# Attention scores on 128 rows: high and low parts of q stacked over k twice, the maximum as one more row

## What is computed

```python
q = conv1x1(Wq)      # (8, 12, 64, 1024)
k = conv1x1(Wk)
v = conv1x1(Wv)
scores = jnp.einsum('bhdn,bhdm->bhnm', q, k) * scale
attn = jax.nn.softmax(scores, axis=-1)
out = jnp.einsum('bhnm,bhdm->bhdn', attn, v)
out = out.reshape(B, C, H, W)
return jnp.einsum('oc,bchw->bohw', Wp, out)
...
x = x + _L0_conv_ref(_gn(x), L0_conv_Wq, L0_conv_Wk, L0_conv_Wv, L0_conv_Wp)
```

## Time and profile before

| | |
|---|---|
| median of 3 runs | 3721.03 us (3720.8 to 3722.98) |
| profiled execution | 3720.18 us |
| its span, first to last instruction | 3718.4 us |
| PE busy in the span | 95% |
| POOL, DVE, ACT busy in the span | 48%, 39%, 31% |
| DMA queue q1, share of 16 engines | 37.1% |
| HBM | 266 MB read, 206 MB written |

### The profile page before, as it was taken

One profiled execution on the slowest core, in us unless ns is written; L12 is line 12 of the kernel. 1 busy time (PEld: TensorE's weight loads), 2 busy tenths in 40 slices (PEclk: granted clock), 3 DMA queues, 4 the chain that ended last, 5 costly groups with the idle time before them and its releaser, 6 DMA issues.

```text
span 3718.4 us, 52007 instructions
## 1 busy us (share of the span) xinstructions
PE 3543.5 (95%) x18800; PEld 2342.1 (63%) x18800; DVE 1443.6 (39%) x1787; ACT 1160.4 (31%) x2017; POOL 1803.1 (48%) x772
## 2 busy tenths in 40 slices
PE   3999999999999888899999999999999999999996
PEld 3888988888889744445555555555555555555555
DVE  4333333233332154444444444444444444444421
ACT  2111111111111034444444444444434444444340
POOL 0000000000000058887777777787777777778770
PEclk7999999999999989999999999999999999999998
DMA  4333324323333332244343443433433434434325
GB/s 188 136 132 124 131 101 145 142 101 133 116 135 105 122 137 92 92 137 137 126 148 112 140 148 114 140 115 116 144 132 131 145 106 148 140 115 139 120 70 169
DMA packets 264948, 476.07 MB, mean 128 GB/s; under 512 B 60704, under 2 KB 110112, under 8 KB 263712
## 3 DMA queue, kind: packets, MB, share of 16 engines
q1 hardware_dynamic: 264736, 473.27, 37.1%
HBM read 265.95 MB, written 206.44 MB: 127 GB/s over the span
## 4 chain that ended last, share of the span: by engine, by line
PE 60%; issue 2%; ACT 2%; DVE 1%; DMA 0%; POOL 0%; POOLq 0%; ACTq 0%; SPq 0%
PE psum L712 23%; PE psum L725 19%; PE psum L745 12%; PE psum L697 5%; ACT p_all L807 2%; PE psum L736 1%; DVE half_max L850 0%; POOL sums L674 0%; DMA k<-k_parts 0%; DMA k<-o_parts 0%; POOL o L657 0%; DMA o_parts<-o_lo 0%; POOLq L409 0%; DMA top<-neg_max 0%; ACTq L806 0%
## 5 line engine op out<-in xcount | busy, mean ns | idle before, releaser
L674 POOL TENSOR_TENSOR sums<-sums,p_all 128x1024 f32<-128x1024 f32 x576 | 1357.8, 2381 | 204.5 <-ACT p_all L807 204.5
L850 DVE TENSOR_REDUCE half_max<-psum 128x2 f32<-128x1024 f32 x768 | 940.4, 1226 | 1266.8 <-PE psum L697 1266.8
L807 ACT ACTIVATE p_all<-psum 128x512 f32<-128x512 f32 x1536 | 834.3, 595 | 1149.1 <-PE psum L712 1140.6
L674 POOL TENSOR_TENSOR sums<-p_all 128x1024 f32<-128x1024 f32 x96 | 226.0, 2375 | 1625.7 <-ACT p_all L807 1625.7
L712 PE MATMUL psum<-q,k 64*128 64x512 f32 x4608 | 742.8, 427 | 52.3 <-ACT p_all L807 50.3
L725 PE MATMUL psum<-p_all,v 128*64 128x512 f32 x3072 | 743.4, 605 | 0.0
L712 PEld LDWEIGHTS psum<-q,k 64*128 64x128 f32 x4608 | 375.2, 185 | 511.7 <-issue 278.8
L745 PE MATMUL psum<-a,wp 128*128 128x512 f32 x1620 | 465.1, 416 | 0.0
L225 PE MATMUL psum<-xn_hi,w_hi 128*128 128x512 f32 x1152 | 449.9, 391 | 5.6 <-DVE xn_lo L334 5.5
L225 PE MATMUL psum<-xn_lo,w_hi 128*128 128x512 f32 x1152 | 449.0, 390 | 0.0
L225 PE MATMUL psum<-xn_hi,w_lo 128*128 128x512 f32 x1152 | 449.0, 390 | 0.0
(11 more groups left out here) (55 smaller groups left out, 2032.3 us busy)
## 6 DMA issues: line engine op xcount, KB each, us to landing
q_parts<-stage SPq DMA_DIRECT2D x192, 256.0 KB, 2.1
k_parts<-stage SPq DMA_DIRECT2D x192, 256.0 KB, 2.3
q<-q_parts SPq DMA_DIRECT2D x48, 1024.0 KB, 6.3
k<-k_parts SPq DMA_DIRECT2D x48, 1024.0 KB, 8.9
a<-o_parts SPq DMA_DIRECT2D x90, 512.0 KB, 5.0
x_raw<-in_x SPq DMA_DIRECT2D x8, 3072.0 KB, 11.2
v_rows<-stage SPq DMA_DIRECT2D x128, 192.0 KB, 2.1
v<-v_rows SPq DMA_DIRECT2D x48, 512.0 KB, 4.2
```

The costliest lines, as they stand in the source:

```text
L674: pool.tensor_tensor(sums[:, m % 2, i, :], first, p_all[:, i, n, :], ALU.add).then_inc(added, 1)
L807: act.activation(p_all[:, i, (m * MT + t) % EXPS, h * BANK:(h + 1) * BANK], scores[:, r, :], ACT.Exp, scale=SCALE).then_inc(exp_done, 1)
L850: dve.tensor_reduce(half_max[:, :, t, h], of, AX.X, ALU.max, negate=True).then_inc(max_done, 1)
```

## The change

Each head gets 128 rows. `q_both` holds the high part of q on 64 rows and the low part on the other 64; `k_twice` holds the high part of k on both; one product of the two gives high k by high q plus high k by low q. `k_low` holds the low part of k on one half, zeros on the other half, and ones in one row of that half; `q_top` holds the high part of q on the same half, zeros on the other, and the maxima in that one row. Their product gives low k by high q plus the maximum. A K block is now 4 matmuls on all 128 rows, 2 for one head, then 2 for the other, and each head waits for its own score bank.

U keeps its form (64 rows a head; the heads' tiles are now `q_top` and `k_twice`), and moves: in steps 2 to 6 one unit stands between the second K and V and one behind V. O stands between the two K blocks without a unit, except in step 7, where a unit splits it. S moves ahead of V. `sums` has one buffer. q and k are loaded by eight DMAs a pair in place of two (3 MB in place of 2 MB), the parts of `lo` one pair ahead, with two slots. At the start DVE sets the zero halves and the rows of ones.

```diff
-    UNITS_BY_STEP = ((1, 1, 1),) + ((0, 1, 1),) * 6 + ((0, 1, 0),)
+    UNITS_BY_STEP = ((1, 1, 0, 1, 0), (0, 0, 0, 0, 1)) + ((0, 0, 0, 1, 1),) * 5 + ((0, 0, 1, 1, 0),)
...
-                ch = bass.ds(p * P, P)
-                sp.dma_start(f32(q[:, e, :, :]), q_dram[:, ch, :].rearrange("s p n -> p s n")).then_inc(qk_in[e], 16)
-                sp.dma_start(f32(k[:, e, :, :]), k_dram[:, ch, :].rearrange("s p n -> p s n")).then_inc(qk_in[e], 16)
+                for i, part in enumerate(half_of):
+                    sp.dma_start(f32(q_top[part, e, i, :]), q_dram[0, bass.ds(p * P + i * DH, DH), :]).then_inc(hi_in[e], 16)
+                for part in half_of:
+                    sp.dma_start(f32(k_twice[part, e, :, :]),
+                                 k_dram[0, bass.ds(p * P, P), :].rearrange("(i c) n -> c i n", i=2)).then_inc(hi_in[e], 16)
+
+            def load_lo(p, e, scored):
+
+                wait(sp, s_ready, scored)
+                for s, part in enumerate(half_of):
+                    sp.dma_start(f32(q_both[part, e, :, :]),
+                                 q_dram[s, bass.ds(p * P, P), :].rearrange("(i c) n -> c i n", i=2)).then_inc(lo_in[e], 16)
+                for i, part in enumerate(half_of):
+                    sp.dma_start(f32(k_low[part, e, i, :]), k_dram[1, bass.ds(p * P + i * DH, DH), :]).then_inc(lo_in[e], 16)
...
                         if t == 1:
-                            wait(pool, sums_ready, p - 1)
+                            wait(pool, sums_ready, p)
...
-                wait(pe, exp_done, n + 2 - RING)
                 cols, keys = slice(h * BANK, (h + 1) * BANK), slice(t * P, (t + 1) * P)
-                for c in range(4):
-                    for i, part in enumerate(half_of):
-                        r = ((m * MT + t) * 4 + 2 * h + i) % RING
-                        left, right = ((k[part, e, 0, keys], q[part, e, 0, cols]), (k[part, e, 0, keys], q[part, e, 1, cols]),
-                                       (k[part, e, 1, keys], q[part, e, 0, cols]), (ones_r[part, :], top[part, e, cols]))[c]
-                        mm = pe.matmul(scores[:, r, :], left, right, start=(c == 0), stop=(c == 3))
-                        if c == 3:
-                            mm.then_inc(s_ready, 1)
+                for i, c in ((0, 0), (1, 0), (0, 1), (1, 1)) if first else ((0, 0), (0, 1), (1, 0), (1, 1)):
+                    r = ((m * MT + t) * 4 + 2 * h + i) % RING
+                    if c == 0:
+                        wait(pe, exp_done, n + i + 1 - RING)
+                    if first and (i, c) == (0, 1):
+                        pe.wait_ge(top_in, 32 * (p + 1))
+                    left, right = ((k_twice[:, e, i, keys], q_both[:, l, i, cols]),
+                                   (k_low[:, l, i, keys], q_top[:, e, i, cols]))[c]
+                    mm = pe.matmul(scores[:, r, :], left, right, start=(c == 0), stop=(c == 1))
+                    if c == 1:
+                        mm.then_inc(s_ready, 1)
...
                 for t in range(MT):
+                    front, behind, middle, late, end = units(t)
+                    maxima(front)
                     if t == 0 and not first:
                         values(p - 1, m - 1, None, MT - 1)
+                    maxima(behind)
+                    scores_by_key(p, m, u, t, 0)
...
+                        output(small, n % KT, share[:2], count)
+                    maxima(middle)
+                    if at_least(p, LAG):
+                        output(small, n % KT, share[2:], count)
+                    scores_by_key(p, m, u, t, 1)
+                    maxima(late)
+                    if t == SUMS_AT and not first:
+                        add_up(p - 1, m - 1, (p + 1) * UNITS + sum(map(sum, UNITS_BY_STEP[:t])) if not last else NP * UNITS)
                     if t > 0:
                         values(p, m, u, t - 1)
+                    if t == SUMS_AT:
+                        wait(pe, sum_copied, p)
+                    maxima(end)
...
-            dve.memset(f32(ones_r[:]), 1.0).then_inc(set_done, 1)
-            dve.memset(f32(top[:]), 0.0).then_inc(set_done, 1)
+            for i in range(2):
+                other, row = half_of[1 - i], slice((1 - i) * DH, (1 - i) * DH + 1)
+                dve.memset(f32(q_top[other, :, i, :]), 0.0).then_inc(set_done, 1)
+                dve.memset(f32(k_low[other, :, i, :]), 0.0).then_inc(low_zero, 1)
+                dve.wait_ge(low_zero, i + 1)
+                dve.memset(f32(k_low[row, :, i, :]), 1.0).then_inc(set_done, 1)
```

More of the change, by code:

```diff
@@ L422, in attend_phase @@
         p_all = sb("p_all", [P, 2, EXPS, N])
[L423 removed]
+        sums = sb("sums", [P, 2, N])
         half_max = sb("half_max", [P, 2, MT, 2])
@@ L505, in units @@
             done = sum(map(sum, UNITS_BY_STEP[:t]))
-            first, second, third = UNITS_BY_STEP[t]
-            return (range(done, done + first), range(done + first, done + first + second),
-                    range(done + first + second, done + first + second + third))
-        SETS = 3
+            ends = [done + sum(UNITS_BY_STEP[t][:n]) for n in range(6)]
+            return [range(a, z) for a, z in zip(ends, ends[1:])]
+        SETS = 5
         block = ctx.enter_context(nc.Block())
@@ L692, in scores_by_query @@
                 if unit == 0:
-                    pe.wait_ge(qk_in[e], 32 * (turn(p, m, u) + 1))
+                    pe.wait_ge(hi_in[e], 64 * (turn(p, m, u) + 1))
                 wait(pe, max_done, p * UNITS + unit if taken is None else taken)
                 for i, part in enumerate(half_of):
-                    queries = q[part, e, 0, :].rearrange("p (n t) -> p t n", t=MT)[:, t, :]
-                    mm = pe.matmul(to[:, i, :], queries, k[part, e, 0, h * BANK:(h + 1) * BANK], start=True, stop=True)
+                    queries = q_top[part, e, i, :].rearrange("p (n t) -> p t n", t=MT)[:, t, :]
@@ L698, in scores_by_query, with scores_by_key @@
+                    mm = pe.matmul(to[:, i, :], queries, k_twice[part, e, i, h * BANK:(h + 1) * BANK], start=True, stop=True)
                 mm.then_inc(rows_ready, 1)
-            def scores_by_key(p, m, t, h):
-                e = m % SLOTS
-                if t == 0 and h == 0:
-                    pe.wait_ge(top_in, 32 * (p + 1))
+            def scores_by_key(p, m, u, t, h):
+                e, l = m % SLOTS, m % Q_SLOTS
+                first = t == 0 and h == 0
+                if first:
+                    pe.wait_ge(lo_in[l], 64 * (turn(p, m, u, Q_SLOTS) + 1))
@@ L735, in add_up @@
                         c, cols = 2 * i + h, slice(h * BANK, (h + 1) * BANK)
-                        mm = pe.matmul(totals[c * QUARTER:(c + 1) * QUARTER, :], ones[:], sums[:, m % 2, i, cols], start=True, stop=True)
+                        mm = pe.matmul(totals[c * QUARTER:(c + 1) * QUARTER, :], ones[:], sums[:, i, cols], start=True, stop=True)
                 mm.then_inc(sums_ready, 1)
@@ L877, in pair @@
                 for t in range(MT):
-                    begun, early, late = units(t) if not last else ((), (), ())
-                    for unit in (*begun, *early):
+                    front, behind, middle, late, end = units(t) if not last else [()] * 5
+                    for unit in (*front, *behind, *middle):
                         unit_max(p + 1, m + 1, unit)
-                    if t == MT - 1 and not last:
-                        join(p + 1, m + 1)
                     if t == RECIP_AT and not first:
@@ L886, in pair @@
                         unit_max(p + 1, m + 1, unit)
+                    if t == MT - 1 and not last:
+                        join(p + 1, m + 1)
                     if t in (HALF_STEP, MT - 1) and at_least(p, LAG):
@@ L889, in pair @@
                         add_x((p - LAG) * 2 + s, s, p - LAG + 1)
+                    for unit in end:
+                        unit_max(p + 1, m + 1, unit)
             all_pairs(dve, pair)
```

59 lines of the change are left out of this document (27 added, 32 removed).

## The result

| | before | after |
|---|---|---|
| median of the runs | 3721.2 us | 4056.9 us (4055.3 to 4063.9) |
| profiled span | 3718.4 us | 4053.5 us |
| mean granted clock | 0.984 | 0.956 |
| q1, share of 16 engines | 37.1% | 44.3% |
| bytes of all queues | 476 MB | 526 MB |

The ratio is 1.0905, with an interval of 1.0886 to 1.0924: slower by 9%, where the text forecast 1.4% and a range that ended at 3800.

A forecast was written before the change was run, and what follows sets the result against it. PE was taken to bound the kernel, so changes in its order count in full: 3720.2 us, +56 for pairs with O, -7 for pairs without, +4.5 at the start, gives 3774 us, range 3745 to 3800.

The forecast's parts named there:

- Part 1, the products: K blocks on PE: 4 slots each before and after, 15.04 us a pair both times, so no gain.
- Part 2, the stretches: PE's runs of one matmul form: fewer stretches but 16 lone units at 0.55 us, +1.4 us a pair, +56 us over 40.
- Part 3, waits: Waits between engines and DMAs: the 0.62 us wait at step 1 goes, new candidates (a) to (d) cost nothing.
- clause (d): Loads of q and k: issued a whole pair ahead, so 1 MB more and six more issues a pair cost nothing.
- Clauses (a) to (c): DVE's maxima, the last unit's row for `q_top`, and the single `sums` buffer: each wait covered, costing nothing.
- The 0.62 us at step 1: PE's wait between U and K in step 1, once a pair: forecast to go, counted in Part 2's sum.
- Clause (b): The last unit's maxima reaching `q_top`: PE has about 6 us of work ahead, cover over 1.5 us, so nothing.
- Rival 4, a chain gets late: Maxima at step 7 or the row of `top` come late: up to 1 us a pair, 3820 us, chance 0.04.
- Rivals 1, 2, 3: U behind K cheaper: 3702, 0.08; long-run slots 0.216 us: 3696, 0.03 (no change 0.03); mid-run K wait: 3849, 0.06.
- rival 3: K's second head waits on `exp_done` mid-stretch, baring 0.1 us of weight load a block: 75 us, 3849 us, chance 0.06.
- Part 5, the start: DVE's settings at the start take 12.2 us in place of 2.8, delaying the first reduction: +4.5 us (0 to 7).

The follow-up runs named there:

- e1: The changed kernel with the eight loads of q and k issued behind the sums' DMAs: 3764.9 us, ratio 1.0118.
- e4: The kernel before with 1 MB more loaded in each pair, into a tile nobody reads: 3722.1 us, ratio 1.0001.
- e9: The kernel before with its 2 MB of q and k a pair in eight DMAs on 64 partitions, in place of two: 3737.6 us, ratio 1.0043.
- e3: The changed kernel with the store of y issued ahead of the eight loads: 3918.6 us, ratio 1.0534.
- e14: e1 with unit weights every 2nd query, the second head's maxima sent by ACT's queue and its tiles set on GpSimd: 3741.5 us, ratio 1.0056.
- e13: e14 with the four loads of `hi` issued by ACT's queue in steps 0 to 3, `lo` still behind the sums: 3700.3 us, ratio 0.9947.

## Why the prediction was wrong

**Part 1, the products: right.** K is 4 slots: away from the gaps, K's rows of the changed kernel follow each other by 0.23 us, against 0.235.

**Part 2, the stretches: right in kind and 0.4 us a pair too high, measured by e1.** A unit alone is 0.55 us behind V and behind K alike:

```profile
2207.70 0.62 PE L713 MATMUL psum<-k_twice,q_top 64*128 64x512 f32 x2
2208.25 1.94 PE L744 MATMUL psum<-p_all,v 128*64 128x512 f32 x8
2210.12 0.62 PE L713 MATMUL psum<-k_twice,q_top 64*128 64x512 f32 x2
2210.67 1.94 PE L744 MATMUL psum<-p_all,v 128*64 128x512 f32 x8
```

(PE's timeline of after: U behind K, then U behind V; against the earlier trace rows.) The period with output came out at 49.7 us in e1, against 50.1 forecast; the slot in a run of 13 is 0.230 rather than 0.235, which on 100 slots is 0.5 us. Over 39 periods e1 has 49.87 us and the kernel before 48.83, +1.0 a pair where the sum had +1.4. Without output it was 43.0 against 42.4 forecast and 43.5 before: the eight-slot run K K takes 2.17 us (1425.81 to 1427.98 in e1) in place of 2.07, since the second head of its second K waits for its bank: the weight load at 1427.31 follows 0.27 us of idle time that ACT's exponentials ended, and the next product comes 0.34 us behind in place of 0.23.

**Part 3, waits: here is the step that failed.** Its clause (d) said of q that it "is issued a whole pair ahead, so the extra 1 MB a pair, and six more issues, cost nothing". It asked who needs the loaded data, and the answer was right: nobody waited for q or k. It didn't ask what stands *behind* the loads in the queue: the store of y, the load that waits for that store, and the sums. The trace of before had the line, in SyncE's own wait list, that I hadn't used:

```profile
SPq L564 <- DMA out<-y: 492.3, 94, 10.2
```

a queue that already stood still 5 us a time for a store. Clauses (a) to (c) held (in e1 no gap has their name). The 0.62 us at step 1 did go. What the clause left out was worth 292 us (e1). Four edits draw on the same cover: 1 MB more (alone nothing, e4), eight DMAs in place of two (alone 16 us, e9), the last unit behind the second K of step 7, which lets the loads begin later, and S one V earlier. Clause (b) weighed that last unit for the row of the maxima alone, and found its cover; that SyncE's loads stand behind those maxima was in no clause. The last two were not run alone, and that the four add up to the 292 us is my reading of the one pair's times, not a run. The sum rule "a cost that is covered is nothing" fails when several edits draw on one cover.

**Rival 4, a chain gets late,** was the right kind with the wrong place and a price of 1 us a pair; it had 0.04. The real gap was 2.1 to 10.5 us, and I had no term for the clock: after the gap shown K O K ran 4.7 us (2238.62 to 2243.30) in place of some 3.2, and by PE's busy time against e1 the clock took 74 us in all.

**Rivals 1, 2, 3: out.** U behind K is not cheaper (0.55). Slots are 0.230 in long runs, not 0.216. K's second head doesn't bare 0.1 us in a run with O; in the runs K K of the six pairs without O it does (above), which is rival 3's mechanism at a price of about 0.6 us a pair.

**Part 5, the start: the settings 3 us too low.** The first reduction began at 1309.4, forecast 1306.4, so 7.5 us later than before and not 4.5: the settings took 0.85 ns an element on 64 partitions and even on one, as assumed, but each is followed by 0.4 to 0.7 us of idle time that I hadn't added. The first K was 7.5 us late too (1330.54 against 1323.05), but S of the first pair only 2.9: the first pair itself, which no part of the sum had, made up 4.6.

## What to carry to other kernels

When an edit makes a transfer larger, splits it or moves it, read what stands behind it in its queue, down to the smallest DMA whose landing an engine waits for, and compare its landing with the time at which it is wanted, in the worst kind of pair and not in the mean. Read also what stands ahead: a wait that ends later lets all that follows it in the queue start later. A wait in that queue for a store is a warning even when no engine shows idle time. And matmuls whose weights are strided by 16 bytes or more belong inside a run of their own form: the slow load is hidden there and bare at the head of a run.

## What was unexpected in the hardware

- Weight loads of 128 fp32 columns have two lengths by the distance of their elements: 183 and 191 ns at 4 and 8 bytes, 304 and 309 ns at 16 and 32.
- Four DMAs of 2 KB landed in 10.6 to 11.5 us behind 3 MB in the same queue (e3), and in about 2 us without.
- DMAs of 1 KB behind 2 MB in flight took 6.0 us in the median, in the queue of the 2 MB and in another alike (e14), and 2.0 where the 2 MB had landed (e13).
- The same 2 MB in eight DMAs put off what stood behind by up to 6.7 us against two (e9), in the pair read above by the time of the issues.
- Setting one partition takes as long as setting 64: 1.76 us for 2048 elements both times.
